# New order of attention, second biases on VectorE, and gates picked by a product, in a kernel of linear attention and routed experts

## The reference

```python
xn = _layernorm(x, axis=-1)
x = x + _L0_attn_ref(xn, Wq, Wk, Wv, Wo) + _L0_ffn_ref(xn, gate_w, gate_b, w1, b1, w2, b2)
# attention, 16 heads of 8, per batch of 256 tokens
Qf = elu(xn @ Wq) + 1 ; Kf = elu(xn @ Wk) + 1 ; V = xn @ Wv      # per head
Kv = einsum('bhlm,bhln->bhmn', Kf, V) ; K1 = sum(Kf, axis=2)
out = (Qf @ Kv) / (Qf @ K1 + 1e-6) ; return out @ Wo
# experts: 8 of them, hidden size 256, the best 2 of each token
probs = softmax(xn @ gate_w.T + gate_b) ; topk_vals, topk_idx = top_k(probs, 2)
h = relu(xn @ w1[e] + b1[e]) ; expert_out[e] = h @ w2[e] + b2[e]
return sum(expert_out[topk_idx] * topk_vals)
```

## Time and profile before

| what | us |
|---|---|
| median of 3 runs | 119.11 (118.44 to 119.73) |
| the profiled execution itself | 117.28 |
| its span, first to last instruction | 115.5 |
| busy: TensorE, ScalarE, VectorE, GpSimd | 97.6, 61.7, 56.0, 51.4 |
| last matmul of attention issued, about | 52.4 |
| last second product ends, about | 108.8 |

### The profile page before, as it was taken

The page is one execution under the profiler, slowest core; times in us unless marked ns, Lnnn a source line. Parts: engine busy times, 40 slices in busy tenths (PEclk is TensorE's granted clock), DMA queues, the critical chain, the costliest instruction groups (busy, mean ns, idle before and its releaser), DMA issues.

```text
span 115.5 us, 2916 instructions
## 1 busy us (share of the span) xinstructions
PE 97.6 (85%) x780; PEld 90.2 (78%) x780; DVE 56.0 (49%) x222; ACT 61.7 (53%) x175; POOL 51.4 (44%) x62
## 2 busy tenths in 40 slices
PE   6948689991875799998999999999999999999600
PEld 6836578570574799987999999999999999999500
DVE  0789579699468475423253333443334433333400
ACT  4359768975031022223857586667766666676300
POOL 5016500477777769010000504123504557887870
PEclk9999999999999999999999999999999999999996
DMA  3995000001213821697446656757586787994522
GB/s 106 283 320 235 3 0 6 0 27 52 73 49 108 250 69 49 164 300 279 114 127 174 134 142 180 149 153 161 162 180 143 168 169 158 184 177 76 45 23 23
DMA packets 16703, 15.06 MB, mean 130 GB/s; under 512 B 1936, under 2 KB 16272, under 8 KB 16560
## 3 DMA queue, kind: packets, MB, share of 16 engines
q1 hardware_dynamic: 13584, 12.50, 36.6%
q0 software_dynamic: 2816, 2.18, 13.7%
q10 hardware_dynamic: 288, 0.20, 0.6%
HBM read 11.64 MB, written 3.23 MB: 129 GB/s over the span
## 4 chain that ended last, share of the span: by engine, by line
issue 28%; PE 23%; POOL 20%; DVE 13%; DMA 6%; ACT 4%; POOLq 2%; SPq 1%
POOL out L474 20%; DMA x_tok<-in_x 4%; PE banks L1037 4%; PE banks L1032 4%; PE banks L1007 4%; PE banks L917 3%; DVE kf L759 2%; PE banks L983 2%; DMA out<-res 2%; ACT xrow L511 2%; POOLq L115 2%; DVE qf L765 2%; PE banks L1018 2%; PE banks L945 1%; ACT xT L517 1%
## 5 line engine op out<-in xcount | busy, mean ns | idle before, releaser
L559 ACT ACTIVATE h<-banks,w_now 128x128 f32<-128x128 f32 x118 | 36.8, 364 | 17.3 <-PE banks L1068 17.3
L474 POOL DMA_INDIRECT out<-acc,token x16 | 25.0, 1562 | 34.5 <-DVE acc L807 33.0
L807 DVE SCALAR_TENSOR_TENSOR acc<-banks,xs,acc 128x128 f32 x59 | 20.7, 351 | 34.8 <-PE banks L1081 33.8
L1068 PE MATMUL banks<-xsT,w_now 128*128 x236 | 36.3, 277 | 0.4 <-issue 0.4
L1081 PE MATMUL banks<-w_all,h 128*128 x236 | 36.0, 276 | 0.0
L1068 PEld LDWEIGHTS banks<-xsT,w_now 128*128 128x128 f32 x236 | 30.9, 192 | 0.9 <-issue 0.8
L1081 PEld LDWEIGHTS banks<-w_all,h 128*128 128x128 f32 x236 | 30.9, 192 | 0.4 <-issue 0.2
L459 POOL DMA_INDIRECT sorted_dram<-xrow,slot x16 | 16.7, 1046 | 5.8 <-issue 4.6
L543 ACT COPY attT<-banks 128x512 f32<-128x512 f32 x4 | 2.3, 585 | 11.7 <-PE banks L1018 11.7
L917 PE MATMUL banks<-wkvg_f,xT 128*128 128x136 f32 x32 | 5.2, 294 | 3.2 <-ACT xT L517 2.6
L917 PEld LDWEIGHTS banks<-wkvg_f,xT 128*128 128x128 f32 x32 | 4.1, 189 | 4.2 <-ACT xT L517 3.0
(11 more groups left out here) (100 smaller groups left out, 111.6 us busy)
## 6 DMA issues: line engine op xcount, KB each, us to landing
w_now<-in_w1b SPq DMA_DIRECT2D x59, 129.0 KB, 2.3
w_all<-in_w SPq DMA_DIRECT2D x1, 1032.0 KB, 5.7
out<-res SPq DMA_DIRECT2D x4, 256.0 KB, 4.2
xs<-sorted_dram SPq DMA_DIRECT2D x3, 276.0 KB, 4.0
x_tok<-in_x SPq DMA_DIRECT2D x3, 256.0 KB, 4.8
xs<-sorted_dram SPq DMA_DIRECT2D x2, 138.0 KB, 2.5
x_tok<-in_x SPq DMA_DIRECT2D x2, 128.0 KB, 2.4
sorted_dram<-xrow,slot POOLq DMA_INDIRECT x16, 2.6
```

The costliest lines, as they stand in the source:

```text
L474: nc.gpsimd.indirect_dma_start(out=out_rows, out_offset=bass.IndirectOffsetOnAxis(ap=token[:, s:s + 1], axis=0), in_=acc[:, s * D:(s + 1) ...
L559: nc.scalar.activation(h[:, i % NH, c, :], h_ps[i % NHP][:, c * P:(c + 1) * P], ACT.Relu, bias=w1_now[:, i % NW, H + c:H + c + 1]).then_in ...
L807: nc.vector.scalar_tensor_tensor(out=mine, in0=y_ps[i % NYP], scalar=xs[:, bass.ds(goff, 1)], in1=mine, op0=ALU.mult, op1=ALU.add).then_in ...
L1068: last = nc.tensor.matmul(h_ps[i % NHP][:, c * P:(c + 1) * P], w1_now[:, i % NW, c * P:(c + 1) * P], xsT[:, bass.ds(toff, P)], start=True, ...
```

## The change

The diff does four things at once.

First, the order. On TensorE all three groups of `rank_rows` come right after the last `project_vg`, ahead of keys and queries; `keys_values`, `numerator` and `project_q` are interleaved in another order; the visits' order and table come late, after `transpose_att(1)` and `project_out(0)`; three late warm-up matmuls become five and stand behind `project_out(3)`. VectorE and ScalarE follow in their own order, and several results use other banks of PSUM.

Second, the biases. `project_out` has no bias product any more. `w2` is longer by 128 columns for each expert, the bias repeated on all partitions, and the load of w2 larger by half a MB; the strip b2 of 64 KB is not loaded. In each visit VectorE adds the bias to the second product (`take_y`), from PSUM into one of two strips in SBUF, and multiplies and adds from there (`accumulate`). The sum of visit i + 1 is issued ahead of the accumulation of visit i.

Third, the gates. The table has no column for them. GpSimd copies the gates of the sorted rows (`take_gates`), TensorE transposes them in two halves of 4 and 16 tiles (`transpose_gates`), VectorE copies that (`keep_gates`), TensorE multiplies it with `is_visit` (`pick_gates`), and VectorE keeps the result (`keep_picked_gates`): one column of gates for each visit. The first half serves visits 0 to 7, the second the others.

Fourth, GpSimd's `give_back` waits for the token numbers and for the base only once, before the first tile; sorted rows are 137 numbers, not 138.

```diff
@@ -749,8 +755,6 @@
-                nc.vector.tensor_tensor(gates[:, LATE, :], gated[:, LATE, 0, :], gated[:, LATE, 1, :], ALU.add
-                                        ).then_inc(gates_dve_done, 1)
@@ -799,12 +803,31 @@
-            def accumulate(i, toff, goff):
+            def keep_gates(half):
+                rows = GATE_TILES[half] * E
+                dve.wait_ge(gatesT_done, half + 1)
+                nc.vector.tensor_copy(gatesT[0:rows, half, :], gatesT_ps[0:rows, :]).then_inc(gatesT_copied, 1)
...
+            def take_y(i, woff):
+
                 dve.wait_ge(l2_done, i + 1)
+                if i >= 2:
+                    dve.wait_ge(acc_done, i - 1)
+                nc.vector.tensor_tensor(y[:, i % 2, :], y_ps[i % NYP], w2_all[:, bass.ds(woff + KC * D, D)], ALU.add
+                                        ).then_inc(y_done, 1)
+
+            def accumulate(i, toff):
+                dve.wait_ge(y_done, i + 1)
+                dve.wait_ge(gate_of_copied, 1 if i < GATE_VISITS[0][1] else 2)
                 mine = acc[:, bass.ds(toff, D)]
                 if i:
                     dve.wait_ge(acc_done, i)
-                nc.vector.scalar_tensor_tensor(out=mine, in0=y_ps[i % NYP], scalar=xs[:, bass.ds(goff, 1)], in1=mine,
+                nc.vector.scalar_tensor_tensor(out=mine, in0=y[:, i % 2, :], scalar=gate_of[:, i:i + 1], in1=mine,
                                                op0=ALU.mult, op1=ALU.add).then_inc(acc_done, 1)
@@ -836,50 +860,58 @@
             for i in range(NI):
-                if i == 0:
-                    copy_xsT(1)
+                if i == 3:
+                    copy_xsT(3)
                 if i == 4:
-                    copy_xsT(3)
-                accumulate(i, toffs[i // LOADS][i % LOADS], goffs[i // LOADS][i % LOADS])
+                    keep_gates(1)
+                if i == 5:
+                    keep_picked_gates(1)
+                if i + 1 < NI:
+                    take_y(i + 1, woffs[(i + 1) // LOADS][(i + 1) % LOADS])
+                accumulate(i, toffs[i // LOADS][i % LOADS])
@@ -984,23 +1017,28 @@
+            def transpose_gates(half):
+
+                pe.wait_ge(gates_done, half + 1)
+                tiles = GATE_TILES[half]
+                pe.wait_ge(xsT_dve, half + 1)
+                nc.tensor.transpose(gatesT_ps[0:tiles * E, :], gates[:, 0:tiles, :].rearrange("p t e -> p (t e)"),
+                                    ident_t[:]).then_inc(gatesT_done, 1)
+
+            def pick_gates(half):
+
+                pe.wait_ge(gatesT_copied, half + 1)
+                a, b = GATE_VISITS[half]
+                rows = GATE_TILES[half] * E
+                nc.tensor.matmul(gate_of_ps[:, a:b], gatesT[0:rows, half, :], is_visit[0:rows, a:b],
+                                 start=True, stop=True).then_inc(gate_of_done, 1)
@@ -1013,29 +1051,24 @@
-                for j in range(4):
-                    nc.tensor.matmul(wo_ps[k][:, j * P:(j + 1) * P], gatesT[:, k * P:(k + 1) * P],
-                                     b2_f[:, j * P:(j + 1) * P], start=(j == 0), stop=False)
@@ -1076,7 +1110,7 @@
-                    pe.wait_ge(acc_done, i - NYP + 1)
+                    pe.wait_ge(y_done, i - NYP + 1)
@@ -1140,8 +1174,16 @@
+                if i == 0:
+                    transpose_gates(0)
                 if i == 1:
                     transpose_rows(2)
+                if i == 2:
+                    pick_gates(0)
+                if i == 6:
+                    transpose_gates(1)
+                if i == 7:
+                    pick_gates(1)
                 if i == 4:
                     transpose_rows(3)
```

More of the change, by code:

```diff
@@ L43, in pair_key, with shape_constants @@
     return (i + BIAS_OF_KEY) * (j + BIAS_OF_KEY)
-def shape_constants(D, E, T, row, wrow):
+def shape_constants(D, E, T, wrow):
     rows = np.arange(D)
@@ L182, in linear_attention_with_pair_sorted_experts @@
         is_visit = sb("is_visit", [P, NI])
-        table = sb("table", [3, NI], I32)
+        table = sb("table", [2, NI], I32)
         xs = sb("xs", [P, T * ROW])
@@ L434, in gate_values @@
                                         ALU.add).then_inc(row_done, 1)
-                nc.gpsimd.tensor_tensor(gates[:, EARLY, :], gated[:, EARLY, 0, :], gated[:, EARLY, 1, :],
-                                        ALU.add).then_inc(gates_done, 1)
             def fill_rows():
@@ L467, in token_numbers, with take_gates @@
                                       ).then_inc(token_done, 1)
+            def take_gates(half):
+                first, end = (0, GATE_TILES[0]) if half == 0 else GATE_TILES
+                if half:
+                    pool.wait_ge(gatesT_done, 1)
+                nc.gpsimd.tensor_copy(gates[:, first:end, :],
+                                      xs[:].rearrange("p (s c) -> p s c", c=ROW)[:, first:end, D + 1:D + 1 + E]
+                                      ).then_inc(gates_done, 1)
             def give_back(s):
+                if s == 0:
+                    pool.wait_ge(token_done, len(XGROUPS))
+                    pool.wait_ge(base_out, 16 * NBLK)
                 pool.wait_ge(acc_done, BOUND[s])
-                pool.wait_ge(token_done, sum(s >= a for a, _ in XGROUPS))
-                pool.wait_ge(base_out, 16 * NBLK)
                 nc.gpsimd.indirect_dma_start(
@@ L543, in copy_attT @@
                 nc.scalar.copy(attT[:, blk_cols(k)], attT_ps).then_inc(attT_copied, 1)
-            def copy_gatesT():
-                act.wait_ge(gatesT_done, 1)
-                nc.scalar.copy(gatesT[:], gatesT_ps).then_inc(gatesT_copied, 1)
             def copy_xsT(n):
@@ L582, in _ @@
             exp_k(0)
-            for b in range(4, 6):
+            for b in range(4, B):
                 copy_v(b)
             exp_k(1)
-            copy_v(6)
-            copy_v(7)
             exp_q(0)
@@ L592, in _ @@
             exp_k(3)
+            copy_attT(0)
             exp_q(2)
             exp_q(3)
-            copy_gatesT()
-            for k in range(NBLK):
+            for k in range(1, NBLK):
                 copy_attT(k)
@@ L838, in _ @@
             shares()
-            choose(0)
-            late_shift()
             pair_starts()
             places(1, slice(0, 4))
+            late_shift()
             finish_k(0)
             finish_k(1)
-            places(2, slice(4, T))
             mask_kv(0)
             finish_q(0)
+            places(2, slice(4, T))
+            mask_kv(1)
+            finish_k(2)
+            divide(0)
+            finish_q(1)
             choose(1)
             late_gates()
-            finish_k(2)
-            visits()
-            mask_kv(1)
+            mask_kv(2)
             finish_k(3)
-            order_visits()
-            finish_q(1)
-            mask_kv(2)
-            keep_table()
-            divide(0)
+            divide(1)
             finish_q(2)
@@ L861, in _ @@
             finish_q(3)
-            divide(1)
+            visits()
             divide(2)
+            order_visits()
+            divide(3)
+            keep_table()
             residual(0)
-            divide(3)
             residual(1)
@@ L985, in keys_values @@
                 last.then_inc(kv_done, 1)
-            def transpose_gates():
-                pe.wait_ge(table_done, 1)
-                pe.wait_ge(gates_done, 1)
-                pe.wait_ge(gates_dve_done, 1)
-                for k in range(NBLK):
-                    last = nc.tensor.transpose(gatesT_ps[:, k * P:(k + 1) * P],
-                                               gates[:, blk_tiles(k), :].rearrange("p t e -> p (t e)"), ident_t[:])
-                last.then_inc(gatesT_done, 1)
+            def transpose_gates(half):
[6 more added lines that the diff above has]
+                pe.wait_ge(gatesT_copied, half + 1)
+                a, b = GATE_VISITS[half]
+                rows = GATE_TILES[half] * E
+                nc.tensor.matmul(gate_of_ps[:, a:b], gatesT[0:rows, half, :], is_visit[0:rows, a:b],
+                                 start=True, stop=True).then_inc(gate_of_done, 1)
             def numerator(k):
@@ L1037, in project_out @@
                     last = nc.tensor.matmul(wo_ps[k][:, j * P:(j + 1) * P], attT[:, t * P:(t + 1) * P], wo_f[:],
-                                            start=False, stop=(j == 3))
+                                            start=True, stop=True)
                 last.then_inc(wo_done, 1)
@@ L1162 @@
     T = x.shape[0] * x.shape[1] // P
-    row = D + 1 + E + 1
+    row = D + 1 + E
     w1 = np.asarray(L0_ffn_w1).transpose(1, 0, 2)
@@ L1171 @@
     w1b[:, :, H:H + H // P] = b1
-    b2_blocks = np.zeros((4, E, 4, D), dtype=np.float32)
-    for t in range(4):
-        b2_blocks[t, :, t] = np.asarray(L0_ffn_b2)
     arrays = {
@@ L1184 @@
         "w2": np.ascontiguousarray(w2.reshape(P, -1)),
-        "b2_blocks": b2_blocks.reshape(4 * E, 4 * D),
-        "consts": shape_constants(D, E, T, row, row_w),
+        "consts": shape_constants(D, E, T, row_w),
     }
```

145 lines of the change are left out of this document (79 added, 66 removed).

## The result

The changed kernel takes 121.6 us (median of 4 runs, 120.44 to 123.64), the kernel before 119.42 beside it (4 runs, 118.44 to 120.17). The ratio is 1.025, with an interval of 1.018 to 1.033: slower, where 117.7 was forecast, and outside the range. Ratios here compare only executions within 1.5% of the fastest of their kernel; medians and ranges are of all.

A forecast was written before the change was run, and what follows sets the result against it. Attention on TensorE, then TensorE's visits, and GpSimd's give-backs at the end were taken to bound the kernel; -4.8 + 0.35 + 1.9 + 1.13 = -1.4 took 117.28 to 115.9, forecast 117.7 us as median, range 116.0 to 119.8.

The forecast's parts named there:

- The clock falls: Rival, chance 0.06: TensorE's wait for rows halves its clock, four visits at 0.89 more each, +2.2 in sum, 121.3 us.
- The 1.8 us between the profiled execution and the median: Profiled execution 117.28 against the runs' median 119.11; the same difference was applied to the forecast 115.9, giving 117.7.
- the stands: TensorE waits for VectorE's copies at the second gate transpose (1.15) and fourth second product (0.75): 1.9 us, once.
- the tail: Accumulations come behind the next visit's sum, 1.13 us later; GpSimd's give-backs carry that to the end unshortened.
- two small instructions: Gate picks and transpose on TensorE: three small instructions counted at 0.11 to 0.13 each, 0.35 us.
- The rows: Sorted rows decide when visits start; SyncE free for their loads at 44.8, 0.95 earlier; third group at 49.5.
- Attention went as worked out: Attention loses the bias matmuls and no longer holds up visits; table at about 41.0, TensorE through near 44.5.
- a rival, at 0.17: Rows no earlier: weight loads, later table or slower scatter eat the 0.95; sum -0.4, 118.7 us; chance 0.17.
- an earlier scatter than forecast: The sixteen indirect DMAs of the scatter were to move 1.25 us earlier, following the slots and gates.
- the 4.8: TensorE transposes the third group of sorted rows at about 49.55 in place of 54.35: 4.8 us gained.
- VectorE keeps up: Sum and accumulation take VectorE 0.81 a visit, below TensorE's 0.89; the adds cost nothing but delay.
- The signs: Wrong if: visits over 0.89 apart awaiting sums; clock under 1.00 after 45; row loads issued after 45; give-backs above 1.87.

The follow-up runs named there:

- second profile: The kernel before, unchanged, profiled once more: 120.3 us (median of four), the profiled execution with a span of 117.0 and a mean clock of 0.958.
- eighteen warm-ups: Changed kernel with 18 late warm-up matmuls behind the last output projection instead of 5: 119.23 us, ratio 1.013 to the kernel before.
- Taken away alone: Changed kernel with the second gate transpose and pick, and VectorE's copies for them, in later visits: 118.09 us, ratio 0.9995 to the kernel before.
- both cures: Changed kernel with 18 late warm-ups instead of 5 and the second gate transpose and pick two visits later: 117.45 us, ratio 1.000 to the kernel before.
- the variants: Follow-ups on the changed kernel: more warm-ups, later second gates, weight loads behind rows, no second bias, accumulation without lag, some combined; medians 116.41 to 121.62 us.
- the filled kernel before: Kernel before with idle multiplications in TensorE's hole ahead of the visits' order: 24 gave 119.42 us, ratio 1.022; 12 gave 119.28 us, ratio 0.991.

## Why the prediction was wrong

- **The clock.** The step that failed is the rival *The clock falls*: the sum put the fall at nothing and the rival had 0.06, because "the trace of before, with the longer wait, does not bear it out". In the changed kernel a wait of 2.88 us was followed by 0.50 for the whole of 50 to 55 us. And the kernel before, with the same wait of 3.12 us, does bear it out in its second profile. One trace of an event that comes or stays away by chance was read as a rule. The page of the Trainium skill cited there ("TensorE: Matmul & The Clock Gate", "HAM oscillation — how this bites in real kernels") says that a wait for a DMA between bursts of matmuls can drop the engine to its half clock. The row at 50 to 55 us agrees with it. With more warm-ups alone the median goes from 121.6 to 119.2 (the kernel before: 119.42 and 119.28 beside them), so this step is worth some 2.4 us of the 3.9 by which the forecast was missed. That the rival's own 121.3 lies so near the 121.6 is in part luck: it priced the fall at 3.6 us, on top of a sum that was too low.
- **The 1.8 us between the profiled execution and the median.** I carried them over as a constant. In the second profile of the kernel before, 1.5 us of the span are the same effect: the lower clock in its attention puts its third group of rows 1.87 later (56.22 against 54.35). The sum started from the kernel before with its clock kept, so it speaks of the changed kernel with its clock kept. That is the profile with eighteen warm-ups, 117.1: +1.6 to the span of before, not -1.4. The 3.0 between them are 0.7 at the first second product (4.0 early instead of 4.7), 1.5 in the stands, 0.4 in later visits and 0.4 in the tail (8.2 against 6.7, forecast +1.1). The 1.8 hid part of this: beside the 119.2 of that kernel the 117.7 is only 1.5 too low.
- **The stands.** The mechanism was right. The waits were 1.39 and 0.54, in sum the 1.9 of the forecast, but by two misses that cancel (1.15 and 0.75 were forecast). Mis-sized was the term. At full clock the three visits cost 3.6 more, where 1.9 and 0.24 for two small instructions stood in the sum: a third wait of 0.41 came on top, and at each wait the piece before it runs out and the next starts anew (0.71 instead of 0.61). Taken away alone, the stands gave 3.5 us, with the second fall of the clock; both cures together gave 4.2 (117.45), so the two overlap.
- **The rows.** Attention went as worked out: the table is kept at 40.26, forecast 41.0. The rows went out at 45.82 in place of 44.8, and at 44.4 to 44.9 in the variants. The scatter's landing was taken as 1.5 us from a kernel in which no other load was under way; it is 2.1 to 2.6 beside the weight loads. This was named as a rival, at 0.17. In the variants an earlier scatter than forecast (its end 1.8 to 2.2 before that of the kernel before, forecast 1.25) made up for it, so there the 44.8 came out by luck. With eighteen warm-ups the rows went out at 44.66; the third group, there at 49.81 and not at 49.5, leaves 4.4 of the 4.8.
- **VectorE and the tail.** 0.24 from sum to accumulation and 0.80 a visit, forecast 0.24 and 0.81: VectorE keeps up. The tail grew by 1.0 in the profile after, and by 1.5 with eighteen warm-ups and 1.4 with both cures, forecast 1.13. GpSimd's queue carried a delay to the end only in the first. With eighteen warm-ups the eighth give-back starts 0.56 later than before and the sixteenth 1.61, since the fourteenth stood 1.15 us for VectorE.
- **The signs.** Two of the four that the prediction named for being wrong came in the profile after: a granted clock under 1.00 after 45 us, and rows issued after 45.
- **Open:** why the same hole keeps the clock in one execution and lowers it in the next, where the executions of the filled kernel before lose their time, and how much of the changed kernel's loss outside its profile is the first fall and how much the second.

## What to carry to other kernels

Before a sum is built on one profiled execution, compare its granted clock and its time with those of the other runs: a gap between the two can be a mechanism, and not an offset. Look at the clock where TensorE has work, since a mean over the span takes in the end. A change that makes TensorE wait for data where it was busy is to be priced with a good chance of the half clock for the work that follows, or given idle multiplications that last until the data come, and no longer (here 18 paid, and 24 in another wait outlasted it). An order that staggers two dependent instructions to hide a wait should be tried without the stagger.

## What the runs showed of the hardware

The same wait of 3.12 us left the granted clock at 1.00 in one execution and lowered it to 0.50 for 5 us in another. SyncE, which waits for the last scatter of 128 rows to land, was let go 2.6 us after its issue had ended with six loads of 129 KB under way, 1.3 without. Where the clock is 1.00 throughout the work, as with eighteen warm-ups, it still falls after the last product, and the mean over the span shows 0.975. On VectorE an accumulation that waits for the sum just ahead of it starts 0.42 us after that sum's start (0.28 long), while a sum that waits for an accumulation stands 0.21 after its end: the cost of a wait between neighbours depends on which one waits.
